# Gated cross attention with a mixture of experts: joint maxima, the query copy on VectorE, and the first stacks issued from two queues

## The reference

```python
qkv = _layernorm(x) @ Wqkv + bqkv
qkv_a = ctx @ Wqkv_aux + bqkv_aux
dots = einsum('bhqd,bhkd->bhqk', q, k) * scale
dots_aux = einsum('bhqd,bhkd->bhqk', q, ka) * scale
p, pa = softmax(dots), softmax(dots_aux)
gate = sigmoid(g)
out = (p @ v) * (1 - gate) + (pa @ va) * gate
x = x + tanh(g_xattn) * (out @ Wo + bo)
x = x + tanh(g_ffn) * experts(_layernorm(x))
```

## Time and profile before

| | us |
|---|---|
| median of 3 runs | 863.81 (863.57 to 864.4) |
| the profiled execution | 864.29 |
| its span, first to last instruction | 861.5 |
| TensorE busy in the span | 825.7 (96%) |
| VectorE | 687.3 (80%) |
| GpSimd | 635.7 (74%) |
| ScalarE | 569.5 (66%) |
| TensorE busy from 20 to 40 us | 12.48 of 20 |

### The profile page before, as it was taken

How to read it: one execution, slowest core, us unless ns; L and a number is a source line. 1 busy time by engine, 2 the same in 40 slices (tenths; PEclk the granted TensorE clock), 3 DMA queues, 4 the chain that set the end, 5 groups by cost and what they waited for, 6 DMA issues and landing times.

```text
span 861.5 us, 20208 instructions
## 1 busy us (share of the span) xinstructions
PE 825.7 (96%) x6739; PEld 632.7 (73%) x6739; DVE 687.3 (80%) x1648; ACT 569.5 (66%) x968; POOL 635.7 (74%) x602
## 2 busy tenths in 40 slices
PE   5699999999999899999999999999999999999997
PEld 3366666666666578888888888878888888888885
DVE  6799899898888769769678887867986967876665
ACT  4388888788878765575566576557567556655553
POOL 2567888878854367877886787777787777788785
PEclk9999999999999999999999999999999999999999
DMA  4677777787662166647545654764754655646552
GB/s 114 167 172 167 167 188 158 175 177 168 153 142 56 52 151 137 152 112 165 135 125 143 138 145 110 158 151 101 158 147 116 161 137 126 154 114 153 135 138 58
DMA packets 107630, 120.02 MB, mean 139 GB/s; under 512 B 28154, under 2 KB 69948, under 8 KB 106092
## 3 DMA queue, kind: packets, MB, share of 16 engines
q1 hardware_dynamic: 104652, 118.23, 57.8%
q10 hardware_dynamic: 2880, 0.59, 0.4%
HBM read 103.55 MB, written 14.71 MB: 137 GB/s over the span
## 4 chain that ended last, share of the span: by engine, by line
PE 82%; DMA 6%; DVE 4%; SPq 3%; issue 2%; ACT 2%; POOL 1%; DVEq 0%; ACTq 0%; POOLq 0%
PE bank L2020 20%; PE bank L2022 20%; PE bank L2021 20%; PE bank L1350 5%; PE bank L1336 4%; PE bank L1305 3%; DMA stack_k<-k_scratch 2%; PE bank L1287 2%; DMA stack_q<-nmaxT 1%; PE bank L1358 1%; DVE mx L1000 1%; SPq L416 1%; SPq L419 1%; PE bank L1371 1%; PE bank L1271 1%
## 5 line engine op out<-in xcount | busy, mean ns | idle before, releaser
L1697 POOL TENSOR_TENSOR hid<-act,cwb 128x512 f32<-128x512 f32 x264 | 422.6, 1611 | 127.6 <-DVE act L1924 64.0
L1750 ACT ACTIVATE silu<-bank 128x512 f32<-128x512 f32 x256 | 152.7, 596 | 185.5 <-PE bank L2022 184.1
L1924 DVE TENSOR_TENSOR act<-silu,bank 128x512 f32<-128x512 f32 (+1 forms) x264 | 180.3, 683 | 112.7 <-ACT silu L1750 76.5
L1932 DVE TENSOR_TENSOR hlo<-hid,hhi 128x512 fp32r<-128x512 f32 x256 | 202.9, 793 | 10.6 <-ACT hhi L1756 10.3
L2020 PE MATMUL bank<-xhi,weights_hi 128*128 128x512 f32 x520 | 206.7, 397 | 0.0
L2022 PE MATMUL bank<-xlo,weights_hi 128*128 128x512 f32 x520 | 204.1, 393 | 0.0
L2021 PE MATMUL bank<-xhi,weights_lo 128*128 128x512 f32 x520 | 203.8, 392 | 0.0
L1756 ACT ACTIVATE hhi<-hid 128x512 fp32r<-128x512 f32 (+1 forms) x264 | 165.1, 626 | 20.7 <-POOL hid L1697 18.6
L1000 DVE TENSOR_REDUCE mx<-bank 128x4 f32<-128x512 f32 x240 | 156.0, 683 | 23.9 <-PE bank L1305 22.6
L795 ACT ACTIVATE prob<-bank 128x1024 f32<-128x1024 f32 x128 | 130.9, 1023 | 42.2 <-PE bank L1336 38.8
L2022 PEld LDWEIGHTS bank<-xlo,weights_hi 128*128 128x128 f32 x520 | 97.5, 188 | 22.0
(11 more groups left out here) (241 smaller groups left out, 991.5 us busy)
## 6 DMA issues: line engine op xcount, KB each, us to landing
cwb<-wts_scratch SPq DMA_DIRECT2D x174, 384.0 KB, 5.4
stack_k<-k_scratch SPq DMA_DIRECT2D x30, 256.0 KB, 4.4
k_scratch<-parts_k SPq DMA_DIRECT2D x15, 384.0 KB, 3.4
stack_q<-q_scratch SPq DMA_DIRECT2D x30, 128.0 KB, 2.9
stack_k<-k_scratch SPq DMA_DIRECT2D x30, 128.0 KB, 5.3
q_scratch<-parts_q SPq DMA_DIRECT2D x15, 192.0 KB, 2.4
xin<-in_x_dram SPq DMA_DIRECT2D x16, 128.0 KB, 2.7
cin<-in_ctx_dram SPq DMA_DIRECT2D x16, 128.0 KB, 2.4
```

The costliest lines, as they stand in the source:

```text
L1697: pool.tensor_tensor(h_buf[k][:], a_buf[k][:], cwb[slot][:, q % GP, :], ALU.mult).then_inc(h_ok, 1)
L1750: act.activation(s_buf[k % RS][:], g_bank[k % 2][:], ACT.Silu).then_inc(s_ok, 1)
L1924: nc.vector.tensor_tensor(a_buf[k % RS][at], s_buf[k % RS][at], u_bank[k % 3][at], ALU.mult).then_inc(a_ok, 1)
L1932: nc.vector.tensor_tensor(hlo[k % RH][:], h_buf[k % RS][:], hhi[k % RH][:].bitcast(F32), ALU.subtract).then_inc(hl_ok, 1)
```

## The change

- Maxima of the two units of a round are taken by one instruction over both banks (`joint_maxima`, 1024 columns), in the loop as for the first batches.
- `turn_max` stands between the sums of the two units of the first round, not behind both. `evac_nmax` stands ahead of the round's maxima.
- `copy_q` in the loop moves from ScalarE to VectorE, behind the first round's maxima of the pair's second batch; `norm_mean` moves there too, behind it.
- Opening: the transfers for the first stacks are spread over SyncE (ten) and ScalarE (six); the last split of pair 1 moves from VectorE to GpSimd; GpSimd clears its second V earlier; the biases are reordered and turned at once, as three rows; `gate_consts` stands between the first maxima; all four rounds of scores of batch 0 are ahead of the next projection.

```diff
-        def maxima(b, par, u):
-            wait(dve, s_mm, UNITS * b + u + 1)
...
+        def joint_maxima(b, r, banks=two_banks):
+            wait(dve, s_mm, UNITS * b + 2 * r + 2)
+            if r == 0:
                 wait(dve, nm_ok, b - 1)
...
+        def copy_q(n):
+            wait(dve, qk_mm, n + 1)
+            wait(dve, lo_ok, SPLITS * (n - 1) + 1)
+            nc.vector.tensor_scalar(full_q[:], misc[0][:, 0:TC].rearrange("p (c t) -> p c t", c=CH),
+                                    bcol[:, 0:1], None, ALU.add).then_inc(q_ev, 1)
...
-                    if two_more:
-                        maxima(b + 2, odd, u)
                     if u == (1 if late else 0) and one_more:
                         evac_nmax(b + 1)
+                    if two_more and u % 2 == 0:
+                        joint_maxima(b + 2, u // 2)
...
-                    if u == 7 and not odd and n + 4 < NC:
+                    if u == 1 and odd and n + 3 < NC:
+                        copy_q(n + 3)
+                    if u == 1 and odd and n + 4 < NC:
                         norm_mean(n + 4)
...
-                    if r == 0 and one_more and not late:
-                        wait(pe, nm_ev, b + 1)
-                        turn_max(b + 1)
+                        if u == 0 and one_more and not late:
+                            wait(pe, nm_ev, b + 1)
+                            turn_max(b + 1)
...
-                    if odd and r == 0 and n + 3 < NC:
-                        copy_q(n + 3)
...
         copy_k(1)
+        load_first_k(act, 0, 1)
         copy_first_ka(1)
+        load_first_k(act, 0, 0)
+        load_first_k(act, 1, 1)
...
-        load_first(0)
+        load_first_q(sp, 0, 1)
         store_first_k(1)
-        load_first(1)
+        load_first_q(sp, 0, 0)
+        load_first_q(sp, 1, 1)
+        load_first_q(sp, 1, 0)
+        load_first_k(sp, 1, 0)
...
-        split(1, 1, 1, 1)
         for r in range(ROUNDS):
-            first_maxima(0, r)
+            joint_maxima(0, r, (wide, two_banks)[r % 2])
+            if r == 0:
+                gate_consts()
...
-        pool.wait_ge(lo_ok, SPLITS * 2)
+        pool.wait_ge(lo_ok, SPLITS * 2 - 1)
+        split(1, 1, 1)
...
         first_scores(0, 0)
         first_scores(0, 1)
+        first_scores(0, 2)
+        first_scores(0, 3)
         pe.wait_ge(v_ev, 1)
         project_one(2, 0, 0)
-        first_scores(0, 2)
-        first_scores(0, 3)
+        first_scores(1, 0)
         project_one(2, 0, 1).then_inc(qk_mm, 1)
-        first_scores(1, 0)
         turn_max(0)
         first_scores(1, 1)
+        first_scores(1, 2)
         project_ka(2, 0)
-        first_scores(1, 2)
         first_scores(1, 3)
```

89 lines of the change are left out of this document (37 added, 52 removed).

## The result

The changed kernel takes 875.23 us in the median of 4 runs (874.21 to 879.19), the kernel before 863.69 beside it: a ratio of 1.0142, 95% interval 1.0115 to 1.0169. It is 11.5 us slower. The forecast was 870.4, so the direction was right and the size was 4.8 us short; 875.2 lies just above the upper end of the range. Which step of the sum failed stands in the part on the prediction. The profiled execution of the changed kernel has a span of 876.4 and is itself 4.0 above the median of its runs; the spans of the others are 871.8 to 873.8. So some 3 of the 14.9 us between the two traces belong to this one execution.

What follows compares the result with a forecast made beforehand. The prediction took TensorE's work and a loop over two pairs through the norm mean, GpSimd and transfers as near-equal bounds. +8.9 (mean), -1.5 (opening), -0.8 (end) gave +6.6, so 870.4 us; own range 866 to 874.5, full range 861.5 to 875.

Steps and rivals of the forecast that it cites:

- What bounds the kernel: Middle of attention: TensorE's own work, 31.2 us per two pairs, and a loop through mean, GpSimd and k transfers, 31.3.
- Norm mean: Attention loop: the mean ends 1.9 us later, lengthening the loop over two pairs; +8.9 us, bounds +1.4 to +15.8.
- D: Time from a pair's start to the end of its norm mean, 8.8 us before, forecast to become 10.7.
- L: Time from GpSimd's first step after the mean to the k stack's landing, taken as 22.5 us on average, unchanged.
- Joint maxima: Attention loop: 0.13 us less per round, 16 us off VectorE, none of it on the path.
- the earlier turn and row copy: Second batch's first round: up to 0.6 us saved before the shift rows are sent, mostly lost; counted as nought.
- Rival 2: Attention loop: TensorE's next scores wait for both banks, which come free together; 876 us, chance 0.10.
- Query copy: Attention loop: 13 copies, 6 us in all, move from ScalarE to VectorE; effect on the time nought.
- Opening: Kernel's start: first stack can land 3.8 us sooner, but later maxima limit the gain; -1.5 us, bounds -3.8 to 0.
- End: Last attention pairs: some six rounds with maxima in the chain lose 0.13 each; -0.8 us, between 0 and -1.5.
- rival 1: Transfers behind GpSimd shrink to their shortest everywhere and the middle costs only +1.4; 862.9 us, chance 0.13.

Runs made afterwards that it cites:

- e5: The kernel before with only the joint maxima in the loop; ratio 1.0107 to the kernel before.
- e11: The kernel before with only the loop's query copy moved to VectorE, behind the first round's maxima of the second batch; ratio 0.9993.
- e10: The kernel before with the opening's edits, none of the loop's, and GpSimd's second expert-weight remainder ahead of the root; ratio 0.9972.
- e1: The changed kernel with the norm mean put back at the end of the pair's first batch; ratio 1.0062 to the kernel before.
- e3: The changed kernel, mean still late, with GpSimd's second expert-weight remainder ahead of the root; ratio 1.0109 to the kernel before.
- e6: The changed kernel with the mean back and the row copy behind the round's joint maximum; ratio 1.0065 to the kernel before.
- e8: As e6, with GpSimd's second expert-weight remainder ahead of the root as well; ratio 1.0052 to the kernel before.
- e9: The kernel before with only the turn of the maxima put between the sums of the first round's two units; ratio 1.0056.
- e2: The kernel before with only the norm mean moved to the first round of the pair's second batch; ratio 1.0080.
- e12: The kernel before with SyncE issuing a pair's expert weights behind the k stack's loads, not ahead of them; ratio 1.0115.
- e13: The kernel before with the opening's edits, query copy on VectorE, GpSimd's second weight remainder ahead of the root, and expert weights issued behind the k loads; ratio 1.0200.
- e15: The kernel before with opening's edits, query copy on VectorE, GpSimd's weight remainder ahead of the root, and one opening clearing written as five; 861.35 us, 0.9974.

## Why the prediction was right or wrong

- **What bounds the kernel** (two loops within 0.5 us of each other; VectorE's place counts more than its load): right. VectorE lost 9 us of work in the middle and the kernel got slower; GpSimd waits for the mean in every pair, TensorE for the landing at 11 of 12 starts.
- **Norm mean, +8.9.** Putting it back takes 8.8 us off the twelve pairs. The agreement is partly luck: D was forecast at 10.7 and is 11.3, L was 22.0 and not 22.5. D is longer since the cut turn had made TensorE's rounds longer: the first batch ends later (D is 9.2 with the mean back, not 8.8), and the projection that the query copy waits for ends 10.5 after the start (97.50 + 1.13 - 88.10), where the forecast had 9.75. The turn itself, forecast to come 0.3 sooner, starts 8.9 after the start of the pair where it started 8.6. And the mean's price is counted from a pace that was already worse. On the kernel before, the same move costs only 1.9 us of the twelve pairs in one trace and 0.8% in the median, as D is 10.1 there.
- **Joint maxima, "none of it on the path", and the earlier turn and row copy, "nought"**: this is the step that failed. The joint maxima alone make the kernel 1.07% slower, the turn alone 0.56%, turn and row copy together 0.68%. The forecast counted work on VectorE (0.13 less a round) and not the place of what stands behind it: ScalarE's next exponentials are queued behind the issue that waits for the row copy. And it gave the turn between the sums no price on TensorE, whose list is full. Together they are 4.5 us of the twelve pairs (194.85 - 190.31). Between the traces the sum had +6.6 and 14.9 was measured: of the 8.3 that it lacked, 4.4 lie in the twelve pairs, 2.5 in the last two, 0.9 in the opening and 0.5 in the expert half. Rival 2 had this as "the joint maxima stall TensorE", 876, with a chance of 0.10: its time was right and its mechanism (scores that wait for both banks) is not what the rows of e5 show, where TensorE waits 23 times for the exponentials in the middle and never for the maxima.
- **Query copy, nought**: right (e11).
- **Opening, -1.5**: the mechanism was right, the maxima's end at 37.40 (37.0) takes the place of the stack's landing. TensorE reaches the third round 1.06 sooner (42.34 against 43.40), S(1) 0.6, and alone it is worth 1.0 [-0.1, 2.2] us. The first matmuls behind the long wait take 0.61 for eight where later ones take 0.40, so a restart 1.8 us sooner is in part 1.8 us more of slow running. The granted clock cannot be leaned on for this stretch: the profile gives 1.00 for it in both kernels and 0.50 from 30 to 38 us in e10, with the same 0.61 for the same matmuls.
- **End, -0.8**: wrong in sign. The last two pairs took 1.7 us more, of which a part is the clock (last point). In the chain of the changed kernel:

```profile
268.58 0.48 DVE f_stats L1057 x2
269.06 1.14 DVE mx L1003
...
270.24 0.39 PE bank L1308 x4
```

  Where statistics of the expert half stand ahead of a round's maxima, TensorE waits for the whole joint maximum, 1.1 us here and in e1, e3, e6 and e8, 0.8 in e5; the longest such wait before is 0.3. From S(13) to S(14) before took 16.1; it is 16.5 in e5 and 16.4 in e9, 16.7 and 16.8 in e3 and e8, where joint maxima and cut turn meet at a granted clock of 1.00, 17.2 and 17.4 in e1 and e6 (clock 0.69 and 0.62 for 4 us from 260 on), and 17.9 in the changed kernel.
- **The transfers absorb the delay** (rival 1): not shown. L is 22.0 with the mean late, 0.5 less than before, but it is 22.0 with the mean back too and 22.1 with the opening alone. In e2, the mean alone, it is 21.8. Nowhere did it fall to its shortest in every pair.
- **A term that nobody had**: the clock. Behind a wait of 1.72 us at pair 5 the granted clock was 0.86 and then 0.71 of full in the two windows from 120 to 128, and the rows show matmuls of the context's values at 1.06 for four where 0.61 is usual; from 127.8 on they are at their usual length again. Pair 5's D is 12.65 in place of 11.29: 1.36 us. The same came behind the start at 258.09 (1.59 us of waiting, clock 0.64 from 260 to 264). In the middle of the kernel before the clock is 1.00 and the longest wait is 1.3. It doesn't explain why this execution is 4 us above its median: its mean clock is 0.996, and that of the other executions 0.995 to 0.998.

The cause of the slowdown is shown where an edit was taken alone: the late mean (e1, e2), the joint maxima (e5), the cut turn (e9). Two things stay open: why the sums behind a turn start later, and what each edit costs in the presence of the others, since the prices don't add.

## What to carry to other kernels

When two bounds lie within 0.5 us of each other, price the place of every moved instruction on each engine that waits behind it, and not the work saved: follow the row copy to the issue on ScalarE, to the exponentials, to TensorE. On the engine that sets the pace, a reordering of the same instructions has a price of its own, here 0.3 us for a turn put inside a run of sums. And where an engine waits for two things, making one of them earlier saves only up to the other: GpSimd's new order was to save 1.0 us and saved 0.1. Before a small edit is judged by its time, look whether the stretches that it doesn't touch have kept their length.

## What was not expected of the hardware

- Four small instructions ahead of a loop took a stall of 7.6 us at its turn, with no releaser in the profile, back to the usual 2.6 behind ScalarE: 0.66% of the kernel, more than any of the gains that were found.
- Two waits of TensorE of 1.6 and 1.7 us in the attention half were each followed by some 4 us of matmuls at up to twice their length, at a granted clock of 0.64 to 0.93 in the windows there. The five waits of 1.9 to 2.9 us in the attention halves of e12 and e13 were too (0.50 to 0.65). But it does not follow from the length alone: behind the same 1.1 us ahead of L1308 near 261 it fell in e1 and e6 and not in e3 and e8, and behind 1.58 us at 182.17 in e15 and 1.72 at 327.04 in the expert half of the changed kernel it stayed at 1.00.
- One turn of 128 by 128 in bf16 between two groups of eight sums lengthened the round by 0.36 us, of which a wait for its operand explains a part.
- The same 384 KB store took 2.5 to 4.9 us in the middle of before, e3, e10, e12 and e13, and the issuing of the load of x 0.43 to 2.94 over all traces.
